# Projection of a long context in a latent-query model: three bundled weight loads, context parts three chunks ahead, key units ordered by fours

## The reference

```python
# four layers l: k and v from the same context (4096 x 256)
q = _split_heads(query @ wq_k + wq_b, H)      # 16 heads of 16 channels
k = _split_heads(key_in @ wk_k + wk_b, H)
v = _split_heads(value @ wv_k + wv_b, H)
logits = jnp.einsum('bhqd,bhkd->bhqk', q, k) / jnp.sqrt(dh)
logits = logits + ((1.0 - mask) * -1e9)[:, None]
attn = jax.nn.softmax(logits, axis=-1) * group_prob[:, None]   # layer 0
out = jnp.einsum('bhqk,bhkd->bhqd', attn, v)
```

## Time and profile before

| | us |
|---|---|
| median of three runs | 1470.7 |
| lowest and highest | 1467.95 and 1472.14 |
| the profiled execution | 1468.63 |
| its span, first to last instruction | 1467.4 |
| busy in the span: PE / DVE / ACT / POOL | 1275.0 / 1017.9 / 851.3 / 479.3 |

### The profile page before, as it was taken

The page is one execution under the profiler, slowest core; times in us unless marked ns, Lnnn a source line. Parts: engine busy times, 40 slices in busy tenths (PEclk is TensorE's granted clock), DMA queues, the critical chain, the costliest instruction groups (busy, mean ns, idle before and its releaser), DMA issues. The chain is left out here.

```text
span 1467.4 us, 29726 instructions
## 1 busy us (share of the span) xinstructions
PE 1275.0 (87%) x10930; PEld 635.7 (43%) x10930; DVE 1017.9 (69%) x2341; ACT 851.3 (58%) x1339; POOL 479.3 (33%) x678
## 2 busy tenths in 40 slices
PE   6689976899999888599999988689998896999987
PEld 5336643233333355233333355324444583444445
DVE  3456866999999634778888244299996235999932
ACT  4332213999999731178888643248888121788862
POOL 1212131789988820434444322011111001111100
PEclk9789987799999997689999999869999997899999
DMA  8268966011114020111114062512226201122400
GB/s 315 72 188 300 286 218 235 19 47 46 37 43 133 2 73 1 49 37 55 55 47 143 2 191 103 160 41 67 56 70 212 73 0 42 50 60 62 123 2 8
DMA packets 115735, 136.62 MB, mean 93 GB/s; under 512 B 13755, under 2 KB 96867, under 8 KB 113516
## 3 DMA queue, kind: packets, MB, share of 16 engines
q1 hardware_dynamic: 107142, 126.55, 27.9%
q10 hardware_dynamic: 8448, 8.17, 1.8%
HBM read 99.73 MB, written 34.90 MB: 92 GB/s over the span
## 5 line engine op out<-in xcount | busy, mean ns | idle before, releaser
L1256 ACT ACTIVATE prob_a<-ps 128x1024 f32<-128x1024 f32 x480 | 468.4, 1019 | 93.9 <-PE ps L1079 57.0
L1061 PE MATMUL ps<-kop,qop 52*128 52x512 f16 x1024 | 302.1, 417 | 65.3 <-DMA qop<-qparts 21.5
L1280 DVE TENSOR_REDUCE best_a<-ps 128x1 f32<-128x512 f32 (+1 forms) x488 | 318.0, 709 | 26.6 <-PE ps L1061 24.7
L1079 PE MATMUL ps<-qop,kop 52*128 52x256 f16 x2048 | 216.8, 279 | 5.9 <-ACT prob_a L1256 2.4
L1108 PE MATMUL ps<-prob_a,vop_a 128*32 128x256 f32 x3072 | 208.4, 392 | 4.7 <-issue 4.7
L1276 DVE CUSTOM_DVE_ANT_0 dump_a<-ps,neg_q 128x512 bf16<-128x512 f32 (+1 forms) x244 | 165.8, 715 | 41.0 <-PE ps L1061 39.8
L1061 PEld LDWEIGHTS ps<-kop,qop 52*128 52x128 f16 x1024 | 73.1, 95 | 247.8 <-DVE best_a L1280 96.6
L1394 POOL TENSOR_TENSOR used_a<-prob_a,gT 128x1024 f32<-128x1024 f32 x64 | 154.0, 2407 | 22.4 <-DVE used_a L1293 17.0
L1372 POOL TENSOR_SCALAR mrest_a<-nmax_a 128x2 f32<-128x2 f32 x64 | 27.7, 434 | 335.0 <-DVE nmax_a L1285 335.0
L1079 PEld LDWEIGHTS ps<-qop,kop 52*128 52x128 f16 x2048 | 92.1, 96 | 103.5 <-issue 50.9
L1108 PEld LDWEIGHTS ps<-prob_a,vop_a 128*32 128x32 f32 x3072 | 84.9, 111 | 87.7 <-issue 54.2
(11 more groups left out here) (382 smaller groups left out, 1785.9 us busy)
## 6 DMA issues: line engine op xcount, KB each, us to landing
kop<-kparts SPq DMA_DIRECT2D x384, 64.0 KB, 2.3
vals<-vst SPq DMA_DIRECT2D x16, 1024.0 KB, 5.7
kparts<-kp SPq DMA_DIRECT2D x64, 256.0 KB, 3.8
vraw<-vals SPq DMA_DIRECT2D x64, 256.0 KB, 3.1
e_w<-in_e_w SPq DMA_DIRECT2D x4, 2048.0 KB, 11.1
z_w<-in_z_w SPq DMA_DIRECT2D x24, 256.0 KB, 7.0
gT<-in_ctxT SPq DMA_DIRECT2D x8, 512.0 KB, 11.3
raw<-in_mask SPq DMA_DIRECT2D x16, 256.0 KB, 3.7
```

Source lines behind the costliest of these rows:

```text
L1061: return pe.matmul(out, qop[rows, h, t * P:(t + 1) * P], kop[rows, h % UNROLL, first:first + CHUNK], start=True, stop=True)
L1079: ins = pe.matmul(st_bank(n)[:, j * NT:(j + 1) * NT], kop[rows, h % UNROLL, at:at + P], qop[rows, h, :], start=(j % 2 == 0), stop=(not add ...
L1256: act.activation(prob[:, n % NP, :], st_bank(n), ACT.Exp, scale=1.0 / SCORE_UNIT).then_inc(S("exp_done"), 1)
L1280: dve.tensor_reduce(out, bank, AX.X, ALU.max).then_inc(sem, 1)
```

## The change

The weights are loaded by four ACT transfers instead of twelve (the first layer of wv by itself, then all of wk, all of wq, and the other three layers of wv), the bias of the values by one instead of four. Units are numbered so that each group of four covers two chunks and both halves. DVE makes three LOW context parts ahead of the first unit and another behind every second unit; ACT makes six HIGH ones ahead and two between the first units. The search for blind rows begins behind unit n = 1, the column is stored behind n = 10 and loaded behind n = 12 instead of behind the layer's end, and POOL clears behind mask 23 instead of 25.

```diff
-CLEAR_AT = 25
+CLEAR_AT = 23
-    FIND_AT = 3
+    FIND_AT = 1
+    AHEAD = 3
+    unit_at = lambda n: (n % 4 // 2, 2 * (n // 4) + n % 2)
...
-                if l == 2:
-                    sp.wait_ge(S("blind_stored"), 16 * QT)
-                    sp.dma_start(blind, c.blind_row.rearrange("n o -> o n").to_broadcast((P, NT))).then_inc(S("blind_loaded"), 16)
+                    if l == 2 and n == FIND_AT + 11:
+                        sp.wait_ge(S("blind_stored"), 16 * QT)
+                        sp.dma_start(blind, c.blind_row.rearrange("n o -> o n").to_broadcast((P, NT))).then_inc(S("blind_loaded"), 16)
...
-                u, mt, j = NK * l + n, n // NCHUNK, n % NCHUNK
+                u, (mt, j) = NK * l + n, unit_at(n)
-                if u < NCHUNK:
+                if l == 0 and mt == 0:
                     pe.wait_ge(S("ctx_low"), j + 1)
...
-                act.wait_ge(S(f"{name}_in{l}"), 16)
+                act.wait_ge(S(f"{name}_in{min(l, 1) if name == 'wv' else 0}"), 16)
...
-            load_weight("wv", 0)
-            for l in range(LAYERS):
-                act.dma_start(bv[:, l, :], c.a["bv4"][l:l + 1, :].to_broadcast((P, D))).then_inc(S("bv_loaded"), 16)
+            load_weights("wv", slice(0, 1))
+            act.dma_start(bv[:, :, :].rearrange("p l n -> p (l n)"),
+                          c.a["bv4"].rearrange("(o l) n -> o (l n)", o=1).to_broadcast((P, LAYERS * D))).then_inc(S("bv_loaded"), 16)
-            for name, l in weights[1:]:
-                load_weight(name, l)
+            load_weights("wk", slice(0, LAYERS))
+            load_weights("wq", slice(0, LAYERS))
+            load_weights("wv", slice(1, LAYERS))
...
-            for j in range(NCHUNK):
+            for j in range(2 * AHEAD):
                 context_high(j)
...
                 high(u)
+                if u < NCHUNK - 2 * AHEAD:
+                    context_high(2 * AHEAD + u)
...
             weight_low("wk", 0)
+            for j in range(AHEAD):
+                context_low(j)
...
-                    if u < NCHUNK:
-                        context_low(u)
...
+                    if l == 0 and n % 2 == 1 and AHEAD + n // 2 < NCHUNK:
+                        context_low(AHEAD + n // 2)
```

More of the change, by code:

```diff
@@ L497, in _ @@
                     sp.wait_ge(S("k_low"), u + 1)
-                    sp.dma_start(c.kparts[l, :, (n // NCHUNK) * P:(n // NCHUNK + 1) * P,
-                                          (n % NCHUNK) * CHUNK:(n % NCHUNK + 1) * CHUNK]
-                                 .rearrange("s p k -> p s k"), kp[:, u % SLOTS, :, :]).then_inc(S(f"k_stored{u % SLOTS}"), 16)
+                    mt, j = unit_at(n)
+                    sp.dma_start(c.kparts[l, :, mt * P:(mt + 1) * P, chunk_cols(j)].rearrange("s p k -> p s k"), kp[:, u % SLOTS, :, :]).then_inc(S(f"k_stored{u % SLOTS}"), 16)
                     if l == 2 and n == FIND_AT + 9:
@@ L605, in _, with load_weights @@
         def _(act):
-            def load_weight(name, l):
-                act.dma_start(w32[name][:, l, :, :], c.a[f"{name}4"][l, :, :].rearrange("(t p) n -> p t n", p=P))\
-                   .then_inc(S(f"{name}_in{l}"), 16)
+            def load_weights(name, layers):
+                act.dma_start(w32[name][:, layers, :, :].rearrange("p l t n -> p (l t) n"),
+                              c.a[f"{name}4"][layers, :, :].rearrange("l (t p) n -> p (l t) n", p=P))\
+                   .then_inc(S(f"{name}_in{layers.start}"), 16)
             def square_weight(i, name, l):
-                act.wait_ge(S(f"{name}_in{l}"), 16)
+                act.wait_ge(S(f"{name}_in{min(l, 1) if name == 'wv' else 0}"), 16)
                 dump = ctxp[:, 0, :, :].rearrange("p t k -> p (t k)")[:, CT * D * i:CT * D * (i + 1)].bitcast(BF16)
@@ L635, in high @@
                 act.activation(kp[:, u % SLOTS, HIGH, :], c.ps[:, K_BANKS[u % 4], :], ACT.Identity,
-                               bias=bk[:, l, n // NCHUNK:n // NCHUNK + 1]).then_inc(S("k_high"), 1)
-            load_weight("wv", 0)
-            for l in range(LAYERS):
-                act.dma_start(bv[:, l, :], c.a["bv4"][l:l + 1, :].to_broadcast((P, D))).then_inc(S("bv_loaded"), 16)
+                               bias=bk[:, l, unit_at(n)[0]:unit_at(n)[0] + 1]).then_inc(S("k_high"), 1)
+            load_weights("wv", slice(0, 1))
+            act.dma_start(bv[:, :, :].rearrange("p l n -> p (l n)"),
+                          c.a["bv4"].rearrange("(o l) n -> o (l n)", o=1).to_broadcast((P, LAYERS * D))).then_inc(S("bv_loaded"), 16)
             act.dma_start(bk[:, :, :], c.a["bk4"]).then_inc(S("bk_loaded"), 16)
@@ L683, in stage_values @@
                 if first == 0 and l == 0:
-                    dve.wait_ge(S("bv_loaded"), 16 * LAYERS)
+                    dve.wait_ge(S("bv_loaded"), 16)
                 for k in range(first, first + n):
@@ L810, in _ @@
                     dve.scalar_tensor_tensor(out=kp[:, u % SLOTS, LOW, :], in0=c.ps[:, K_BANKS[u % 4], :],
-                                             scalar=bk[:, l, n // NCHUNK:n // NCHUNK + 1],
+                                             scalar=bk[:, l, unit_at(n)[0]:unit_at(n)[0] + 1],
                                              in1=kp[:, u % SLOTS, HIGH, :],
                                              op0=ALU.add, op1=ALU.subtract).then_inc(S("k_low"), 1)
+                    if l == 0 and n % 2 == 1 and AHEAD + n // 2 < NCHUNK:
+                        context_low(AHEAD + n // 2)
                     if l == 2:
```

## The result

The changed kernel takes 1445.4 us (median of four executions, 1443.9 to 1448.4) beside 1470.1 for the one before: ratio 0.9835, 95% interval 0.9811 to 0.9858. The forecast was 1444.4. The profiled execution took 1446.9, its span is 1445.7. DVE, ACT and POOL are as busy as before. PE is busy for 17.0 us less (1258.0): 10.0 of them lie in the projection (185.4 against 195.4), where more of its work runs at the upper clock level. The other 7.0 lie behind it, where the trace has 75 matmul records fewer (9753 against 9828) for the same code, so they are no gain.

What follows compares the result with a forecast made beforehand. It took layer 0's serial chain, with TensorE waiting for context parts, as the worst stretch. Layer 0 -23.8, start +2.0, blind row 0 and -4.5 sum to -26.3 us: 1444.4 against the median 1470.7, range 1436 to 1457.

Steps and rivals of the forecast that it cites:

- Layer 0: Projection's first layer: context parts leave the chain, 16 units run at TensorE's pace, 26.4 us against 50.2, -23.8 us.
- The detour: Layer 0, ahead of unit 4: turning and copying x, then projecting the query, 5.1 us.
- The start: Before the first unit: wq lands as one bundle, delaying squares, scales and first unit; +2.0 us, bounds -2 and +9.
- idle 1 to 3 us before its sixth square: Sign of being right at the start: ScalarE waits 1 to 3 us for wq.
- The blind row: Layers 2 and 3: earlier search and reload bring the first factor forward; -4.5 us, bounds -7.3 and 0.
- Rival (d): Around layer 2's end: the jam of four-byte stores holds the queue, making the kernel slower, 1482 us at 225 GB/s; 3%.
- The stall by the clearing: Layer 3: GpSimd clears for 8 us and VectorE's product behind the first factor meets it as now.
- (a): Whole stage: transfers take back part of the gain; at 255 GB/s it takes 182.4 us, total 1457; 15%.
- (b): Layer 0: TensorE stays at 1.2 GHz for much of it; half the units slow, 10.4 us, about 1455; 7%.
- (c): Start: bundled weights land together, +9, 1451, 13%; or in good time, -2, 1440, 7%.
- (e): Layer 0: another chain of equal length replaces the old one, still 4 us a unit, 1468 to 1472; 3%.
- One sign of being wrong: Projection stage: ScalarE waiting on stores for more than 5 us in all.

Runs made afterwards that it cites:

- run 1: The kernel before with only the lead of three context parts, units in their old order: ratio 0.9836 to the kernel before.
- run 2: The kernel before with only the order of units by fours, each context part still made on demand: ratio 0.9971 to the kernel before.
- run 4: The changed kernel with the blind-row part taken back (search, clearing and reload as before): ratio 0.9823 to the kernel before.
- run 7: The changed kernel with the clearing moved from GpSimd to VectorE, behind its last factor: ratio 0.9774 to the kernel before.
- run 9: The changed kernel with the blind row made by two TensorE matmuls and a ScalarE copy, without HBM stores and reload: ratio 0.9733 to the kernel before.
- run 3: The kernel before with only the three bundled weight loads and the single bias load: ratio 1.0002 to the kernel before.
- run 5: The changed kernel with ScalarE's squares in the order in which the weight bundles land: ratio 0.9815 to the kernel before.
- run 6: The changed kernel with each mask factor waiting only for its own mask, not for all: ratio 0.9810 to the kernel before.
- run 12: The changed kernel with landing-order squares, per-factor masks, VectorE clearing, TensorE blind row, masks one unit earlier and 20 idle matmuls before the barrier: 0.9673 to the kernel before.

## Why the prediction came out as it did

**Layer 0** (predicted -23.8, measured -26.1). The mechanism was right: 16 units of 1.30 us. The detour was mis-sized: I took 5.1 us from a row at 1.2 GHz, it took 3.1 (from 53.44 to 56.53) at a granted clock of 1.00, and the 0.5 us for the second part did not appear. Runs 1 and 2 show which half of the edit does it: the lead, not the order.

**The start** (+2.0, measured 0.0 in this profile). The mechanism was right, the one semaphore does delay the sixth square and with it the sum. The step that was mis-sized is the landing of wq: I took it at 27.65 less 0.6, and held that "earlier issuing by ScalarE buys nothing". wq was issued at 3.20 instead of 12.45 and landed at 25.1, so the sum came only 0.6 us later. Whether the earlier issue or the bias in longer runs brought it forward is not shown. The value matmuls behind the sum then made up the 0.6: 32 of them in 8.55 us, where the profile of before has them in 9.1. That was chance, since in runs 4, 7 and 9 they took 9.4 to 9.8 us and the first unit started at 49.0 to 49.4. So by run 3 and these traces the term lies between 0 and +1.5, and run 5 shows that the squares did bound the start. The sign "idle 1 to 3 us before its sixth square" failed too (5.8 us): it left out that ScalarE is free 5.3 us earlier. The Trainium skill ("SBUF — State Buffer", The DMA setup-cost knee) would coalesce for speed; by run 3 that brings nothing measurable here.

**The blind row** (-4.5, measured -0.9 to -1.4). Mask 24 was late next, as said. The size failed in "with 3 us of its own it is made from 188 on, and by 193.2 as now if the jam stays". The mask was issued 2.4 us into the layer, as forecast (184.3 is 2.7 in), but it took 10.2 us from there, as it had before, and not 3 behind a queue of 3.8. An issue that is 1.6 us later in the layer and the same 10.2 us can't give 193.2 as now; in the times of before it was made at 194.8, later than the latest time I gave it. The jam moved along with the stores, and the first factor came at the same distance into the layer but for 0.5 us. Rival (d) named the right place. Its jam cost no loss, but it was what held the beginning of layer 3, as runs 6 and 9 show: take one wait away and the next transfer is late; take the stores, the reload and SyncE's wait between them away, and the hole is gone but for 0.7 us. The Trainium skill ("DMA: Bandwidth & Descriptors", Specifications) has 512 bytes as the least size for line rate; the trace agrees in so far as with stores of four-byte elements the median landing of the key stores is 9.8 us and without them 3.7; no run has another size.

**The stall by the clearing** stayed, as predicted. Runs 7 and 12 show it from both sides: GpSimd's mask instruction of 0.62 us took 4.88 in run 12, beside VectorE's clearing of 4.42. The Trainium skill ("SBUF — State Buffer", Who interferes with whom) says the first to issue holds the shared port for the whole instruction; the trace agrees in both directions.

**The total.** The projection gained 27.5 us, 1.2 more than forecast; the medians differ by 24.7. The profiled pair loses 5.8 us behind the projection. Across the profiles of all fourteen kernels that rest takes 1219 to 1229 us with the same code, and the first attention 341 to 348 at a clock of 0.94 to 0.92. The timed gains of the twelve runs lie from 3 below to 11 us above the projection's own, so no giving back is shown. It is not excluded either: the four profiles without the changed kernel's code as a whole (before, runs 1 to 3) have 1219.5 to 1222.0, the ten others 1219.1 to 1229.5. Against it speaks that the kernel before itself took 1465.9 to 1482.7 us in the 23 executions beside runs 1 to 4, at a granted clock of 0.939 to 0.920, so one and the same code varies by more than that. What decides between 1219 and 1229 stays open. That the forecast hit within about 1 us is in part luck: layer 0 and the start were 4.4 us better than forecast, layer 3 some 3.6 worse, and the 5.8 us behind the projection were in no term.

**Rivals.** (a) did not happen: layers 1 and 2 held 83.33 us at 284 GB/s, and the stage from 48.1 on took 170.5 us at 272 GB/s. (b) did not: layer 0 had a granted clock of 1.00. In five of the other profiles it had 0.93 to 0.94 and took 25.4 to 25.7 us, so a slow stretch costs 1.5 us there, not 10. (c) fell on both sides, (e) too. One sign of being wrong did appear, ScalarE waiting on key stores for more than 5 us in all: 16.8 us from layer 0 to layer 3. It was a poor sign, since the kernel before has 11.2 us of it and TensorE stood still for none of the 9.1 us in layers 1 and 2.

## What to carry to other kernels

When an operand is made on demand in an in-order queue, ask behind what it stands; a lead of a few items removes the wait, and reordering its users without a lead does not. If a wait goes and another of equal length takes its place, look for the one transfer that all late ones stand behind; here it was a column of 256 elements of four bytes and the wait for it. Move an instruction that shares a port to where its neighbour is idle, and then look again at what ends last.

## What the runs showed of the hardware that I had not expected

The clearing of 128x4096 fp16 takes 7.98 us on GpSimd and 4.42 on VectorE. ScalarE's issue of its loads ended at 13.5 us with six of them and at 18.8 with seventeen. The later ones took longer to issue: of the seventeen, loads of 256 KB took 0.6 to 0.9 us each up to 8.7 us and 1.8 to 1.9 from the next on, and the last of the six alone took 8.89. TensorE's clock falls to 1.2 GHz at the start of the attention whether TensorE idled for 6.9 us ahead of it or for 2.3; in the second case it falls some 2 us into the attention.
